# Feed-forward opening: the first two weight tiles arrive through a tile shared with the scan, and half of the tokens goes first on VectorE and TensorE

## The reference

```python
x = L0_attn_x
x = x + 0.5 * _L0_ffn_ref(_layernorm(x, axis=-1), L0_ffn_w1, L0_ffn_s1, L0_ffn_w2, L0_ffn_s2, L0_ffn_w3, L0_ffn_s3)
x = x + _L0_attn_ref(_layernorm(x, axis=-1), ...)          # the scan
x = x + 0.5 * _L0_ffn_ref(_layernorm(x, axis=-1), ...)     # same weights
...
def _L0_ffn_ref(x, w1, s1, w2, s2, w3, s3):
    W1 = dequant_q40(w1, s1, hidden, dim)      # 4-bit values times one scale per 64
    W3 = dequant_q40(w3, s3, hidden, dim)
    W2 = dequant_q40(w2, s2, dim, hidden)      # hidden = 1376, dim = 512
    a = jnp.einsum('bsd,hd->bsh', x, W1)
    b = jnp.einsum('bsd,hd->bsh', x, W3)
    h = jax.nn.silu(a) * b
    return jnp.einsum('bsh,dh->bsd', h, W2)
```

## Time and profile before

| what | value |
|---|---|
| time, median of 3 runs | 2438.72 us (2435.86 to 2439.78) |
| profiled execution, its own time | 2434.77 us |
| span of that execution, first to last instruction | 2433.0 us |
| TensorE busy | 2322.9 us, 95% of the span |
| VectorE, ScalarE, GpSimd busy | 1653.1, 1308.2, 1337.8 us |
| mean granted TensorE clock | 0.989 |
| first feed-forward stage, first instruction | 10.73 us |
| second feed-forward stage, first instruction | 1825.45 us |

### The profile page before, as it was taken

One profiled execution on the slowest core, in us unless ns is written; L12 is line 12 of the kernel. 1 busy time (PEld: TensorE's weight loads), 2 busy tenths in 40 slices (PEclk: granted clock), 3 DMA queues, 4 the chain that ended last, 5 costly groups with the idle time before them and its releaser, 6 DMA issues. The chain is left out here.

```text
span 2433.0 us, 33409 instructions
## 1 busy us (share of the span) xinstructions
PE 2322.9 (95%) x12530; PEld 1799.7 (74%) x12530; DVE 1653.1 (68%) x2131; ACT 1308.2 (54%) x1911; POOL 1337.8 (55%) x879
## 2 busy tenths in 40 slices
PE   7998899999999999999999999999988998889878
PEld 6877788888888888888888888888767875545434
DVE  5556887688588578678668758858736544667624
ACT  2323776477467467567657647747732313325544
POOL 2222598599489579669759859948942220100000
PEclk9999999999999999999999999999989999999999
DMA  5422333233223233333323323323215320200001
GB/s 132 107 77 64 104 120 103 88 102 117 83 93 120 87 101 104 100 96 101 107 87 113 104 78 113 112 83 100 83 39 114 90 76 14 82 2 3 2 2 49
DMA packets 163631, 204.09 MB, mean 84 GB/s; under 512 B 24492, under 2 KB 86320, under 8 KB 163344
## 3 DMA queue, kind: packets, MB, share of 16 engines
q1 hardware_dynamic: 162096, 201.43, 28.0%
q10 hardware_dynamic: 1376, 0.53, 0.1%
HBM read 198.43 MB, written 3.15 MB: 83 GB/s over the span
## 5 line engine op out<-in xcount | busy, mean ns | idle before, releaser
L2008 POOL TENSOR_TENSOR mamba_w_lo<-mamba_raw,mamba_w_hi 128x512 fp32r<-128x512 f32 x272 | 436.1, 1612 | 282.9 <-ACT mamba_w_hi L1828 282.9
L76 PE MATMUL psum<-mamba_hT_lo,mamba_w_hi 128*128 128x512 f32 x1152 | 459.4, 399 | 1.8 <-DVE mamba_bc L2100 1.8
L78 PE MATMUL psum<-mamba_hT_hi,mamba_w_lo 128*128 128x512 f32 x1152 | 457.7, 397 | 0.0
L77 PE MATMUL psum<-mamba_hT_hi,mamba_w_hi 128*128 128x512 f32 x1152 | 454.2, 394 | 0.0
L2027 POOL TENSOR_SCALAR mamba_L<-mamba_A,mamba_ts 128x256 f32<-128x256 f32 (+1 forms) x256 | 333.9, 1318 | 0.1
L2132 DVE TENSOR_TENSOR mamba_L<-mamba_L,mamba_cb 128x1536 f32<-128x1536 f32 x128 | 302.6, 2364 | 21.6 <-ACT mamba_L L1877 15.8
L2100 DVE SCALAR_TENSOR_TENSOR mamba_hid<-psum,mamba_cw,mamba_hid 128x1022 f32<-128x1022 f32 (+2 forms) x192 | 245.2, 1277 | 19.8 <-ACT mamba_hid L1835 15.3
L77 PEld LDWEIGHTS psum<-mamba_hT_hi,mamba_w_hi 128*128 128x128 f32 x1152 | 216.5, 188 | 51.4
L76 PEld LDWEIGHTS psum<-mamba_hT_lo,mamba_w_hi 128*128 128x128 f32 x1152 | 216.5, 188 | 51.3 <-DVE mamba_bc L2100 2.0
L78 PEld LDWEIGHTS psum<-mamba_hT_hi,mamba_w_lo 128*128 128x128 f32 x1152 | 216.3, 188 | 51.5
L296 POOL TENSOR_TENSOR ffn_w_lo<-ffn_deq,ffn_w_hi 128x512 fp32r<-128x512 f32 (+2 forms) x66 | 86.2, 1307 | 268.9 <-ACT ffn_w_hi L308 268.9
(11 more groups left out here) (279 smaller groups left out, 4886.8 us busy)
## 6 DMA issues: line engine op xcount, KB each, us to landing
mamba_A<-mamba_a_dram SPq DMA_DIRECT2D x128, 512.0 KB, 4.5
mamba_raw<-in_win SPq DMA_DIRECT2D x144, 256.0 KB, 2.6
mamba_raw<-in_wout SPq DMA_DIRECT2D x128, 256.0 KB, 2.6
mamba_Eb<-mamba_e_dram SPq DMA_DIRECT2D x128, 128.0 KB, 3.0
ffn_raw<-in_w SPq DMA_DIRECT2D x80, 128.0 KB, 3.7
ffn_scl<-in_s SPq DMA_DIRECT2D x76, 128.0 KB, 3.9
ffn_scl<-in_s SPq DMA_DIRECT2D x86, 64.0 KB, 2.4
ffn_raw<-in_w SPq DMA_DIRECT2D x20, 256.0 KB, 2.7
```

The source lines that it names most:

```text
L76: e.matmul(out, wh, ml, start=start, stop=False)
L77: e.matmul(out, wh, mh, start=False, stop=False)
L78: return e.matmul(out, wl, mh, start=False, stop=stop)
L2008: e.tensor_tensor(w.lo[:, k % NSPLIT, :], raw[:, k % NRAW, :], w.hi_read[:, k % NSPLIT, :], ALU.subtract).then_inc(s["w_lo"], 1)
```

## The change

1. **A shared tile.** `raw` (two slots) and `scl` (two slots) of the feed-forward stage and `raw` (four slots) of the scan become views of one tile `ring` of four slots that lives from the start of the program to the first routed stage. The table of shifts becomes such a tile too and is loaded once.
2. **Early loads.** `first_weights` issues the eight DMAs of weight tiles 0 and 1. SyncE calls it in the program's first block, between the first half of `x` and the second, and at the end of the scan stage, after it has waited for all of that stage's low parts. In the first block SyncE's order is now identity, `x` in two quarters, shifts, the eight weight DMAs, second half of `x`; the shifts count on the same semaphore as the identity and the first quarter, for which VectorE's first statistics wait (from 32 to 48). The stage's own loop starts at u = 2, and ScalarE issues no DMA.
3. **VectorE's order.** dequantize(0) comes ahead of `low_rows(0)`, which is no longer cut in two; all four statistics stand together after dequantize(1); dequantize(2) and (3) come ahead of `normalise(1)`.
4. **ScalarE's order.** split(2) and split(3) come ahead of `high_rows(1)`.
5. **TensorE's order.** product(1,0,0) comes ahead of `turn(1)`, and product(1,1,0) behind it, ahead of the wait for all `hT.lo`; then products (0,0), (0,1), (1,0), (1,1) of half 1. `turned` takes banks 1, 3, 5, 7 in place of 4 to 7, and `formed` gives the new counts. `keep_clock` issues 10 + 16 transposes in place of 14 + 24, into bank 0.

```diff
+def first_weights(e, g):
+    ring, d = g["ring"], g["dram"]
+    for n, s in enumerate(("1", "3")):
+        rv, sv = (t.rearrange("p (a n) -> p a n", a=DT) for t in (ring[:, n, :].bitcast(I32), ring[:, 2 + n, :]))
+        for half in range(2):
+            hs = slice(64 * half, 64 * half + 64)
+            e.dma_start(rv[hs], d["w" + s][:, :, 0:P]).then_inc(g["first"][n], 16)
+            e.dma_start(sv[hs], d["s" + s][half, :, 0:P].partition_broadcast(64)).then_inc(g["first"][n], 16)
...
+        raw, scl, shifts = g["ring"][:, 0:2, :].bitcast(I32), g["ring"][:, 2:4, :], g["shifts"]
...
+        def formed(f, h):
+            return 2 * h + f + 1 if f < 2 else 2 * f + h + 1
         def turned(t):
-            return 4 + t % 4
+            return 1 + 2 * (t % 4)
...
-                for u in range(NW):
+                for u in range(2, NW):
...
                 normalise(0)
+                dequantize(0)
+                low_rows(0)
+                dequantize(1)
                 if g["late"]:
                     e.wait_ge(*g["late"])
-                statistics(left[:-2])
-                low_rows(0, 0, 2)
-                e.wait_ge(sh_in, 16)
-                dequantize(0)
-                low_rows(0, 2, 4)
-                dequantize(1)
-                statistics(left[-2:])
+                statistics(left)
                 ch.wait()
                 variances(e, ch, g, 1).then_inc(var_ready, 1)
+                dequantize(2)
+                dequantize(3)
                 normalise(1)
                 low_rows(1)
-                dequantize(2)
-                dequantize(3)
...
-                        e.wait_ge(b_done, n + 1)
+                        e.wait_ge(b_done, formed(f, h))
...
                 high_rows(0)
-                split(0)
-                split(1)
+                for u in range(4):
+                    split(u)
                 high_rows(1)
-                split(2)
-                split(3)
...
-                keep_clock(e, ps[3], ident, 14)
+                keep_clock(e, ps[0], ident, 10)
                 turn(0)
-                keep_clock(e, ps[3], ident, 4)
                 for t in range(HALF_T):
                     e.wait_ge(hT_lo, t + 1)
-                    keep_clock(e, ps[3], ident, 4)
-                keep_clock(e, ps[3], ident, 4)
+                    keep_clock(e, ps[0], ident, 4)
                 product(0, 0, 0)
                 product(0, 1, 0)
+                product(1, 0, 0)
                 turn(1)
+                product(1, 1, 0)
                 e.wait_ge(hT_lo, NT)
-                product(0, 0, 1)
-                product(0, 1, 1)
-                for f in range(1, FT):
+                for f in range(2):
+                    for m in range(2):
+                        product(f, m, 1)
+                for f in range(2, FT):
...
-        raw = c_.sb("raw", [P, NRAW, 512])
+        raw = g["ring"]
...
+                e.wait_ge(s["w_lo"], len(plan.tiles))
+                first_weights(e, g)
...
+                e.dma_start(g["shifts"][:], d["shifts"]).then_inc(loaded[0], 16)
+                first_weights(e, g)
                 e.dma_start(g["x"][:, NT // 2:, :], xv[:, NT // 2:, :]).then_inc(loaded[2], 16)
-                e.wait_ge(loaded[0], 32)
+                e.wait_ge(loaded[0], 48)
...
-                        e.wait_ge(loaded[t // 2], 32 - 16 * (t // 2))
+                        e.wait_ge(loaded[t // 2], 48 - 32 * (t // 2))
```

More of the change, by code:

```diff
@@ L132, in q4_ffn @@
     HALF_T = NT // 2
+    g["stage"] += 1
+    first_in = 64 * g["stage"]
     with ExitStack() as ctx:
@@ L145, in q4_ffn @@
         sil = c.sb("sil", [P, 2, SEQ])
-        sh_in, shifted, deq_ready, w_hi, w_lo, a_done, b_done, silued, hf_ready, hh_hi, hh_lo, w_used, o_done, \
-            x_done, var_ready, rstd_ready, xn_ready, t_done, hT_hi, hT_lo, ahead, ahead_set, dve = (c.sem(s) for s in ("sh_in", "shifted", "deq_ready", "w_hi", "w_lo", "a_done", "b_done",
+        shifted, deq_ready, w_hi, w_lo, a_done, b_done, silued, hf_ready, hh_hi, hh_lo, w_used, o_done, \
+            x_done, var_ready, rstd_ready, xn_ready, t_done, hT_hi, hT_lo, ahead, ahead_set, dve = (c.sem(s) for s in ("shifted", "deq_ready", "w_hi", "w_lo", "a_done", "b_done",
                                          "silued", "hf_ready", "hh_hi", "hh_lo", "w_used", "o_done", "x_done",
@@ L166, in arrived @@
         def arrived(u):
-            return 16 * sum(loads(v) for v in range(u % 2, u + 1, 2))
+            return 16 * sum(loads(v) for v in range(2 + u % 2, u + 1, 2))
+        def formed(f, h):
+            return 2 * h + f + 1 if f < 2 else 2 * f + h + 1
         def turned(t):
-            return 4 + t % 4
+            return 1 + 2 * (t % 4)
         def view(t, u):
@@ L194, in _ @@
                             e.dma_start(rv[hs], d["w" + s][:, :, f * P:f * P + r]).then_inc(raw_in[n], 16)
-                            if u:
-                                e.dma_start(sv[hs], d["s" + s][half, :, f * P:f * P + r].partition_broadcast(64)
-                                            ).then_inc(raw_in[n], 16)
+                            e.dma_start(sv[hs], d["s" + s][half, :, f * P:f * P + r].partition_broadcast(64)
+                                        ).then_inc(raw_in[n], 16)
                     else:
@@ L219, in normalise, with low_rows @@
                                         ALU.subtract, ALU.mult).then_inc(xn_ready, 1)
-                def low_rows(h, first=0, end=HALF_T):
-                    for t in range(h * HALF_T + first, h * HALF_T + end):
+                def low_rows(h):
+                    for t in range(h * HALF_T, (h + 1) * HALF_T):
                         sl = (slice(None), slice(None), slice(t * P, (t + 1) * P))
@@ L231, in dequantize @@
                     r, n = (P, u % 2) if m < 2 else (rows(f), u % 2)
-                    e.wait_ge(raw_in[n], arrived(u))
+                    if u < 2:
+                        e.wait_ge(g["first"][u], first_in)
+                    else:
+                        e.wait_ge(raw_in[n], arrived(u))
                     parts = [(view(raw[:, n, :], u), 0)] if m < 2 else \
@@ L314, in high_rows @@
                                ).then_inc(hT_hi, 1)
-                e.dma_start(shifts[:], d["shifts"]).then_inc(sh_in, 16)
-                m, f = tile(0)
-                for half in range(2):
-                    hs = slice(64 * half, 64 * half + 64)
-                    e.dma_start(view(scl[:, 0, :], 0)[hs], d["s1"][half, :, 0:rows(f)].partition_broadcast(64)
-                                ).then_inc(raw_in[0], 16)
                 high_rows(0)
-                split(0)
-                split(1)
+                for u in range(4):
+                    split(u)
                 high_rows(1)
-                split(2)
-                split(3)
                 for f in range(FT):
@@ L332, in _ @@
                         n = 2 * f + h
[L333 removed]
+                        e.wait_ge(a_done, formed(f, h))
                         if f:
@@ L2305, in build @@
         g["left"], g["late"] = range(NT // 2, NT), (loaded[2], 16)
+        weights = ExitStack()
+        g["ring"] = weights.enter_context(nc.sbuf_tensor("s_ring", [P, 4, 512], F32))[:]
+        g["shifts"] = weights.enter_context(nc.sbuf_tensor("s_shifts", [P, 5, 2], I32))
+        g["first"], g["stage"] = [c.sem(f"first{n}") for n in range(2)], 0
         xv = d["x"].rearrange("(t p) n -> p t n", p=P)
@@ L2334, in build @@
             g["out"] = out.rearrange("(t p) n -> p t n", p=P) if n == len(stages) - 1 else None
+            if s == "routed":
+                weights.close()
             STAGES[s](nc, g, f"{s}{n}_")
```

9 lines of the change are left out of this document (2 added, 7 removed).

## The result

| | median of runs, us | lowest to highest | runs | ratio to before, 95% interval |
|---|---|---|---|---|
| before | 2439.39 | 2433.20 to 2442.43 | 7 | 1 |
| after | 2420.98 | 2419.84 to 2430.09 | 7 | 0.994 (0.9925 to 0.9955) |

The changed kernel is faster by 11 to 18 us, 14.6 at the ratio's middle. The forecast was a gain of 6.35 and a time of 2432.4 (2427.5 to 2438.0). The profiled execution of after took 2424.6 us with a span of 2422.8, against 2434.77 and 2433.0 before. Busy shares by its page: TensorE 96%, VectorE 68%, ScalarE 54%, GpSimd 55%.

A forecast was written before the change was run, and what follows sets the result against it. TensorE, busy 95%, was taken as the bound, waiting within feed-forward stages only in their openings. Gains 1.9 - 1.6 + 6.05 = 6.35 us from 2438.72 gave 2432.4 us, range 2427.5 to 2438.0.

The forecast's parts named there:

- the last sentence of the first opening: Rest of the first feed-forward stage: no wait before and the same matmuls per f, so no further gain or loss.
- First opening: Start of the first feed-forward stage: first product at 8.1 us, the 1.89 us wait for the second half gone; gain 1.9 us.
- go on as long: First opening: with ten transposes for 14, the slow ones last as long, so the last cast ends about 6.1, before 6.45.
- the added wait: First opening: TensorE stands 1.9 us ahead of product(1,0,0) for weight tile 2, with `turn(1)` behind it.
- Second opening: Start of the second feed-forward stage: weights already landed, TensorE's 4.3 us wait gone; gain 7.75, or 6.05 with one clock fall.
- the term kept for the clock: Second opening: one fall to half clock, costing 1.7 us, stays because a wait of about 1.9 us stays.
- rival 1: No clock fall in the second opening (2430.7 us), or shifts at no cost besides (2429.1); chance 0.20.
- First block: Program's start: VectorE's first statistics wait for the shifts until 6.95, making the whole block 1.6 us late.
- Rival 2: Both openings: GpSimd's inverse deviation stalls tile 2's shift, `deq` 1.4 us later, TensorE's wait 3.3; 2435.2 us; chance 0.11.
- Rival 3: Clock falls at both first products and the first opening's third, 5.1 us more: 2437.5 us; chance 0.13.
- Rival 4: First block: shifts land behind weights and second half of `x`, engines start 9.8 us late: 2440.6 us; chance 0.05.
- rival 5: First weights absent at the second stage's start, or gain lost at a later weight tile: 2438.5 us; chance 0.06.

The follow-up runs named there:

- the scan run with 96 and 64 bytes: After, with unused tiles of 96 and 64 bytes in the scan, `hT` and `w` 256 apart, `w` and `zs` 128: 2412.47 us (ratio 0.9909).
- The experiment on the gate: After, with the shifts counted on the semaphore of the first weights, so VectorE's first statistics do not wait for them: 2420.34 us (ratio 0.9945).

## Why the prediction was wrong

**The step that failed** is the last sentence of the first opening: "Before, no wait stood in the rest of the stage, and each f has the same matmuls as before." Both halves are true, and the conclusion was not: the same matmuls took 0.2267 us each in place of 0.2333 in the output part. That is 1.56 us in each of two stages, 3.12 in all, at a place that the sum did not have. The experiments show the cause. It could have been seen: the removed tile of shifts is in the diff, and in the profile of before the products of the same stage already stood at 0.2267 (72 in 16.40 us is 0.2278 with their handovers) beside 0.2333 in the output part. I read waits, and not rates.

**First opening, forecast 1.9, measured 3.28: mis-sized.** Two terms. The one is that the transposes at half pace "go on as long". In before 22 transposes were slow (0.21 us from start to start, then 0.11), for 4.7 us from the first of them; in after 14, for 3.0 us. So the casts ended 5.25 us after the stage's first instruction and not 6.1, and the first product started a microsecond sooner than forecast. That was in part luck. `turn(0)` took 2.28 us in after; here it is in before's profile, and then in that of the scan run with 96 and 64 bytes, whose opening is after's:

```profile
13.77 2.68 PE L353 MATMUL psum<-s_ident,ffn_xn 128*128 128x128 f32 x16
```

```profile
14.61 3.62 PE L357 MATMUL psum<-s_ident,ffn_xn 128*128 128x128 f32 x16
```

In the second of these 27 were slow and the first product started at 8.4 of its stage. In the eight profiles with after's opening 14 to 27 were, and the time to the last silu grew with them, from 127.41 to 128.59 us. With 22, as in before, it was 128.15 (the run with the shifts off the first statistics), a gain of 2.5. So some 0.7 of the 1.4 us over the forecast come from the moment at which the transposes became fast. The rest is the other term, the added wait, which was 1.21 and not 1.9. The fourth product followed `turn(1)` at 18.95 in place of 20.3.

**Second opening, forecast 6.05, measured 7.97.** The placing of the work gave 7.75, and that was right within 0.2 (6.9 to 8.5 over the other pairs of profiles without a fall in after's opening). What failed is the term kept for the clock: "I keep one such fall in the sum, since a wait of that length stays". The wait was 1.63 against 1.89, and the clock stayed at 1.00, here and behind this wait in all eight profiles. A fall in one stage and none in the other at equal waits was no ground to carry it over; rival 1 had this right, and its second half, shifts at no cost, wrong. A fall can still come elsewhere: in the run with the shifts off the first statistics the clock was granted at 0.50 for 3.4 us from 1822.2, at the head of the second stage behind the barrier, and the way to the last silu took 130.6 us there against 129.2 to 129.7 in the seven others.

**First block, forecast -1.6, measured -1.57**: right in size, and in the released instruction (7.04 for 6.95). The experiment on the gate shows the reason right: the wait for the shifts costs 1.5, and a second quarter that can land later adds 0.1 in this profile and up to 1.1 in others. The Trainium skill (DMA: Bandwidth & Descriptors, Queues, rings and completion order) has each DMA engine take descriptors in ring order; the trace agrees in so far as the shifts landed behind both quarters, 0.27 to 0.32 us behind the second in all eight profiles with this gate (0.3 was forecast).

**The rivals.** Rival 2 is refuted, and in both orders. In the first opening the shift of tile 2 started at 23.40, ahead of GpSimd's 23.58, and kept its 0.54; it was GpSimd that stretched, from 1.64 to 1.87. In the second GpSimd started first, and neither stretched:

```profile
1832.15 0.55 DVE L252 TENSOR_SCALAR s_ring<-s_ring,s_shifts 128x512 int32<-128x512 int32 x1 [0.30 <-DMA s_ring<-in_s]
```

```profile
1831.92 1.64 POOL L101 TENSOR_TENSOR s_rstd<-s_ve,s_nhalf 128x8 f32<-128x8 f32 x1 [1.13 <-DVE s_ve L96]
```

Rival 3 (falls at both first products and at the first opening's third) is refuted by the three stretches at 1.00 and by the full pace of the first opening's products. The Trainium skill (TensorE: Matmul & The Clock Gate, Part 4: PE-mode transpose) does not count transposes as busy time of the array in the same way; the trace disagrees once more, if these are the transposes that the page means (the profile names them matmuls): 42 of them, with one gap of 0.73 us, led to a first product at full clock. Rival 4 is refuted by 7.04; rival 5 by a stage without waits for weights from the fourth product on.

**In sum**: 12.9 us gained without the last stretch, forecast 6.35. The 6.6 us between are 3.1 of the output parts, 1.4 of the first opening, 1.9 of the second, and 0.2 of the rest. The 3.1 are sure to 0.02; the 1.4 and the 1.9 are of one pair of profiles, and between other pairs each gain came out up to 1.2 smaller or 0.5 larger.

## What to carry to other kernels

Where TensorE is busy without a wait, compare the start-to-start time of the same matmul in different stages and before and after an edit; a tile added, dropped or resized moves every tile behind it. Try letting the stationary and the moving fp32 operand start at the same place modulo 256 bytes; expect less than the rate says where other work fills the gap (12.6 of 33 us in the scan). Before a reorder, ask whether the data are there: tile 2 ahead of the statistics waited 2.61 us for its load. Compare several profiles before reading half a microsecond. And test a reordering with the loads that it needs: apart, the two parts of this change gave next to nothing in the first stage.

## What the hardware showed unexpectedly

- A 128x512 fp32 matmul stands at 0.2267 us when its two operands start 0 or 256 bytes apart, at 0.2333 when 64 or 96 apart modulo 256, and at 0.2323 when 128: 2.9% of TensorE's pace, with the same granted clock and no wait in the trace. That it is the addresses is shown in both directions; the mechanism is not.
- GpSimd's inverse deviation (128x8) grows from 1.64 to 1.87 us when a VectorE shift starts 0.17 ahead of it. When GpSimd starts first, by 0.01 to 0.22 us, neither grows (four profiles). Beside a low part of a weight tile (128x512) that started first, the shift does grow, from 0.54 to 1.17, and ends 0.28 behind it.
- At the program's first transposes the number of slow transposes was 14 to 27 over eight profiles of the same opening, which moved the end of the stage's products by 1.2 us.
